# A selective-scan layer with a router: the sum over states as products of 512 moving columns in place of transposed blocks

## The reference

```python
resid_norm = resid * rsqrt(mean(resid * resid, -1) + EPS) * norm_w
skip = resid_norm @ W_skip                      # 512 -> 1024
x_in = resid_norm @ W_in                        # 512 -> 1024
x = silu(conv(x_in, 4 taps) + conv_b)
delta = softplus(x @ W_delta_1 @ W_delta_2 + b_delta_2)
Bm, Cm = x @ W_B, x @ W_C                       # 16 states each
def step(h, inp):                               # over the 2048 positions
    d_l, B_l, C_l, x_l = inp
    h = h * exp(d_l[:, :, None] * A) + (d_l * x_l)[:, :, None] * B_l[:, None, :]
    return h, einsum('ben,bn->be', h, C_l)      # the sum over states
y_skip = (y + x * W_D) * silu(skip)
return resid + y_skip @ W_out
```

## Time and profile before

| | |
|---|---|
| time before, median of 3 | 2380.34 us (2379.85 to 2382.69) |
| the profiled execution | 2379.91 us, its span 2378.0 us |
| PE busy | 1958.7 us (82%), 11717 records |
| POOL busy | 1913.5 us (80%) |
| DVE busy | 1795.4 us (75%) |
| ACT busy | 1669.1 us (70%) |
| mean granted clock of TensorE | 0.939 |
| DMA share | 56.9% of 16 engines |

### The profile page before, as it was taken

One profiled execution on the slowest core, in us unless ns is written; L12 is line 12 of the kernel. 1 busy time (PEld: TensorE's weight loads), 2 busy tenths in 40 slices (PEclk: granted clock), 3 DMA queues, 4 the chain that ended last, 5 costly groups with the idle time before them and its releaser, 6 DMA issues. The chain is left out here.

```text
span 2378.0 us, 35550 instructions
## 1 busy us (share of the span) xinstructions
PE 1958.7 (82%) x11717; PEld 1584.2 (67%) x11717; DVE 1795.4 (75%) x3105; ACT 1669.1 (70%) x3276; POOL 1913.5 (80%) x1192
## 2 busy tenths in 40 slices
PE   5577777898889898898889898898889988797883
PEld 3456666777667676777667686776667776666551
DVE  3377877798697977888697977889697887887522
ACT  2368686877769685787779686786868687787421
POOL 1279898898789797989879897998879898999512
PEclk9988988999999999999999999999999999999996
DMA  4555556665747565674657556574757646555320
GB/s 159 169 178 182 189 177 215 201 216 157 225 151 239 180 215 183 203 229 150 210 175 235 196 186 215 185 228 148 232 169 222 194 154 207 181 183 160 120 71 18
DMA packets 239281, 434.31 MB, mean 183 GB/s; under 512 B 19134, under 2 KB 135418, under 8 KB 239098
## 3 DMA queue, kind: packets, MB, share of 16 engines
q1 hardware_dynamic: 239098, 432.04, 56.9%
HBM read 347.57 MB, written 84.41 MB: 182 GB/s over the span
## 5 line engine op out<-in xcount | busy, mean ns | idle before, releaser
L608 POOL TENSOR_TENSOR hc<-h,c_all 128x1024 f32<-128x1024 f32 x512 | 1205.0, 2365 | 219.5 <-DVE h L953 160.0
L953 DVE TENSOR_TENSOR_SCAN h<-operand,carry,bank 128x512 f32<-128x512 f32 x480 | 597.1, 1271 | 174.1 <-PE bank L1129 142.7
L1134 PE MATMUL y_sum<-ident,hc 128*128 128x128 f32 x4096 | 624.7, 281 | 13.0 <-POOL hc L608 12.7
L1129 PE MATMUL bank<-ident,u_t 128*128 128x128 f32 x2560 | 417.3, 288 | 243.2 <-DVE h L953 219.7
L722 ACT ACTIVATE u_t<-dx_t,b_t 128x256 f32<-128x256 f32 x1280 | 575.0, 499 | 0.5 <-PE bank L1129 0.5
L1129 PEld LDWEIGHTS bank<-ident,u_t 128*128 128x128 f32 x2560 | 312.4, 148 | 375.1 <-issue 240.2
L1134 PEld LDWEIGHTS y_sum<-ident,hc 128*128 128x128 f32 x4096 | 506.1, 146 | 79.8 <-issue 50.2
L592 POOL TENSOR_TENSOR operand<-dx_q,b_all 128x1024 f32<-128x1024 f32 x192 | 454.5, 2367 | 11.0 <-DMA b_all<-bc_dram 11.0
L703 ACT ACTIVATE bank<-delta_q,neg_a 128x512 f32<-128x512 f32 x384 | 262.5, 684 | 263.1 <-DVE h L953 262.7
L703 ACT ACTIVATE operand<-delta_q,neg_a 128x512 f32<-128x512 f32 x640 | 432.9, 714 | 0.0
L953 DVE TENSOR_TENSOR_SCAN h<-bank,carry,operand 128x512 f32<-128x512 f32 x288 | 354.9, 1270 | 33.1 <-POOL operand L592 16.4
(11 more groups left out here) (124 smaller groups left out, 2009.3 us busy)
## 6 DMA issues: line engine op xcount, KB each, us to landing
c_all<-bc_dram SPq DMA_DIRECT2D x256, 512.0 KB, 4.3
b_all<-bc_dram SPq DMA_DIRECT2D x192, 256.0 KB, 5.2
win<-in_L_attn_W_in SPq DMA_DIRECT2D x64, 512.0 KB, 5.7
wskip<-in_L_attn_W_skip SPq DMA_DIRECT2D x64, 512.0 KB, 6.2
x_dram<-x SPq DMA_DIRECT2D x64, 256.0 KB, 4.5
delta_dram<-delta SPq DMA_DIRECT2D x32, 512.0 KB, 7.3
dx_dram<-dx SPq DMA_DIRECT2D x32, 512.0 KB, 7.3
delta_q<-delta_dram SPq DMA_DIRECT2D x32, 512.0 KB, 5.8
```

Source lines behind the costliest of these rows:

```text
L608: nc.gpsimd.tensor_tensor(hc[:, number % 3], h[:, number % 3], c_all[:, j % 2, s % 2:s % 2 + 1].to_broadcast([P, 2, SPAN]), ALU.mult).then ...
L953: nc.vector.tensor_tensor_scan(h[:, number % 3, q], first, second, start, ALU.mult, ALU.add).then_inc(scan_done.sem, 1)
L1129: last = transpose(bank[:, q, b * P:(b + 1) * P], u_t[:, j % 2, b, q * P:(q + 1) * P], ident[:])
L1134: return matmul(to, lhsT=of, rhs=ident[:], is_transpose=True, start=start, stop=stop, skip_group_check=True)
```

## The change

`y_sum` is kept in [e, l]. The identity is the stationary operand and hc moves, 512 columns for each q, as a plain product; x * W_D is the product of diag_d (stationary) with x_q, 512 columns. y_out and y_dram are in [e, l] too, so the part of a chunk is a slice of 256 positions, and `acc` needs no transposes any more: they go, with the signal `y_turned`. DVE writes the gate over the skip product in the bank `routed`, and `ys` is routed * acc; the SBUF tile `gate` goes. What waited for `gate_ready` on PE (the next pair's skip product, the transposes of h2 and dx into routed) now waits for `ys_ready`, as does SP's load of acc two pairs on. ACT's waits on gate_ready stay.

```diff
@@
-    y_dram = nc.dram_tensor("y_dram", [2, 2, PAIRS, P, TB, QE], F32).ap()
+    y_dram = nc.dram_tensor("y_dram", [2, PAIRS, P, 2, SPAN], F32).ap()
@@
-        acc = sb("acc", P, 2, TB, QE)
-        thg, gate = sb("thg", P, 2, 2, T), sb("gate", P, 2, 2, T)
+        acc = sb("acc", P, 2, 2, T)
+        thg = sb("thg", P, 2, 2, T)
@@ load_acc
-                    if v := due(sp, y_turned, t, p - 1):
-                        sp.wait_ge(y_turned.sem, v)
-                    sp.dma_start(acc[:, p % 2], y_dram[chunk // 2 % 2, chunk % 2, p]).then_inc(
+                    if v := due(sp, ys_ready, t, p - 1):
+                        sp.wait_ge(ys_ready.sem, v)
+                    sp.dma_start(acc[:, p % 2], y_dram[chunk // 2 % 2, p, :, :, chunk % 2 * T:(chunk % 2 + 1) * T]).then_inc(
                         acc_loaded[p % 2].sem, 16)
@@ store_y
-                    sp.dma_start(y_dram[stage % 2, :, quarter].rearrange("h p b e -> p h b e"),
-                                 y_out[:].rearrange("p (h b) e -> p h b e", h=2)).then_inc(y_stored.sem, 16)
+                    sp.dma_start(y_dram[stage % 2, quarter], y_out[:]).then_inc(y_stored.sem, 16)
@@ take_y
-                    for pair in range(2):
-                        part = slice(2 * pair, 2 * pair + 2)
-                        nc.scalar.activation(y_out[:, part], y_sum[:, part], ACT.Copy,
-                                             scale=0.5).then_inc(y_read.sem, 1)
+                    for q in range(2):
+                        nc.scalar.activation(y_out[:, q], y_sum[:, q], ACT.Copy, scale=0.5).then_inc(y_read.sem, 1)
@@ DVE, mix
-                                        if v := due(dve, ys_ready, t, p - 1):
-                                            dve.wait_ge(ys_ready.sem, v)
                                         nc.vector.scalar_tensor_tensor(
-                                            out=gate[:, p % 2].rearrange("p e t -> p (e t)"),
-                                            in0=thg[:, p % 2].rearrange("p e t -> p (e t)"), scalar=1.0,
+                                            out=routed[:], in0=thg[:, p % 2].rearrange("p e t -> p (e t)"), scalar=1.0,
                                             in1=routed[:], op0=ALU.add,
                                             op1=ALU.mult).then_inc(gate_ready.sem, 1)
-                                    if s == 3 * p + 16:
-                                        if v := due(dve, y_turned, t, p + 1):
-                                            dve.wait_ge(y_turned.sem, v)
+                                        if v := due(dve, acc_loaded[p % 2], t, p // 2 + 1):
+                                            dve.wait_ge(acc_loaded[p % 2].sem, v)
@@
                                         nc.vector.tensor_tensor(
-                                            ys[:, 2 * p:2 * p + 2, :].rearrange("p e t -> p (e t)"), mixed[:],
-                                            gate[:, p % 2].rearrange("p e t -> p (e t)"),
+                                            ys[:, 2 * p:2 * p + 2, :].rearrange("p e t -> p (e t)"), routed[:],
+                                            acc[:, p % 2].rearrange("p e t -> p (e t)"),
                                             ALU.mult).then_inc(ys_ready.sem, 1)
@@ add_y
-                        for b in (2 * pair, 2 * pair + 1):
-                            for q in range(2):
-                                last = matmul(y_sum[:, b, q * P:(q + 1) * P], lhsT=x_q[:, q, b * P:(b + 1) * P],
-                                              rhs=diag_d[:, 2 * quarter + q], start=b % 2 == 0 and q == 0,
-                                              stop=False, skip_group_check=True)
+                        last = matmul(y_sum[:, q], lhsT=diag_d[:, 2 * quarter + q], rhs=x_q[:, q], start=True,
+                                      stop=False)
@@
-                    for b in (2 * pair, 2 * pair + 1):
-                        for q in range(2):
-                            last = add_turned(y_sum[:, b, q * P:(q + 1) * P], hc[:, number % 3, q, b * P:(b + 1) * P],
-                                              False, n == N - 1)
+                    last = matmul(y_sum[:, q], lhsT=ident[:], rhs=hc[:, number % 3, q], start=False, stop=n == N - 1)
@@ PE, skip product
-                                    if v := due(pe, gate_ready, t, p):
-                                        pe.wait_ge(gate_ready.sem, v)
+                                    if v := due(pe, ys_ready, t, p):
+                                        pe.wait_ge(ys_ready.sem, v)
@@ PE, slot 3p + 15
-                                if s == 3 * p + 15 and not late:
...
-                                    for e in range(2):
-                                        for b in range(TB):
-                                            last = transpose(mixed[:, (2 * e + b) * P:(2 * e + b + 1) * P],
-                                                             acc[:, p % 2, b, e * P:(e + 1) * P], ident[:])
-                                    last.then_inc(y_turned.sem, 1)
```

More of the change, by code:

```diff
@@ L169, in build @@
         carry = sb("carry", P, N, ET)
-        y_out = sb("y_out", P, SB, QE)
-        acc = sb("acc", P, 2, TB, QE)
-        thg, gate = sb("thg", P, 2, 2, T), sb("gate", P, 2, 2, T)
+        y_out = sb("y_out", P, 2, SPAN)
+        acc = sb("acc", P, 2, 2, T)
+        thg = sb("thg", P, 2, 2, T)
         ys = sb("ys", P, ET, T)
@@ L187, in build @@
         bank = stack.enter_context(nc.psum_tensor("bank", [P, 2, SPAN], F32))
-        y_sum = stack.enter_context(nc.psum_tensor("y_sum", [P, SB, QE], F32))
+        y_sum = stack.enter_context(nc.psum_tensor("y_sum", [P, 2, SPAN], F32))
         mixed, routed = (stack.enter_context(nc.psum_tensor(n, [P, 512], F32)) for n in ("mixed", "routed"))
@@ L239, in build @@
         gate_ready = signal("gate_ready", "mix", PAIRS)
-        y_turned, ys_ready = signal("y_turned", "mix", PAIRS), signal("ys_ready", "mix", PAIRS)
+        ys_ready = signal("ys_ready", "mix", PAIRS)
         xp_loaded, z0_ready = loads_of("xp_loaded", "mix", 1), signal("z0_ready", "mix", TB)
@@ L1131, in turn_u, with add_y @@
                     last.then_inc(ut_turned.sem, 1)
-                def add_turned(to, of, start, stop):
-                    return matmul(to, lhsT=of, rhs=ident[:], is_transpose=True, start=start, stop=stop,
-                                  skip_group_check=True)
-                def add_y(t, s, pair):
+                def add_y(t, s, q):
                     if not (now := slot_of(t, s)):
@@ L1143, in add_y @@
                     if n == 0:
-                        if t == -FIRST and k == 0 and pair == 0:
+                        if t == -FIRST and k == 0 and q == 0:
                             pe.wait_ge(diag_made, ET)
@@ L1147, in add_y @@
                             pe.wait_ge(xq_loaded.sem, v)
-                        if v := due(pe, y_read, t, 2 * k - 2 + pair + 1):
+                        if v := due(pe, y_read, t, 2 * k - 2 + q + 1):
                             pe.wait_ge(y_read.sem, v)
-                        for b in (2 * pair, 2 * pair + 1):
-                            for q in range(2):
-                                last = matmul(y_sum[:, b, q * P:(q + 1) * P], lhsT=x_q[:, q, b * P:(b + 1) * P],
-                                              rhs=diag_d[:, 2 * quarter + q], start=b % 2 == 0 and q == 0,
-                                              stop=False, skip_group_check=True)
-                        if pair:
+                        last = matmul(y_sum[:, q], lhsT=diag_d[:, 2 * quarter + q], rhs=x_q[:, q], start=True,
+                                      stop=False)
+                        if q:
                             last.then_inc(xq_read.sem, 1)
@@ L1174, in turn_dx @@
                     if k:
-                        for read, step in ((gate_ready, t - 1), (o_ready, t - 1)):
+                        for read, step in ((ys_ready, t - 1), (o_ready, t - 1)):
                             if v := due(pe, read, step, read.per):
@@ L1319, in side_work @@
                                         last.then_inc(skip_done.sem, 1)
-                                if s == 3 * p + 15 and not late:
-                                    if v := due(pe, acc_loaded[p % 2], t, p // 2 + 1):
-                                        pe.wait_ge(acc_loaded[p % 2].sem, v)
-                                    if v := due(pe, z_ready, t - 1, TB):
-                                        pe.wait_ge(z_ready.sem, v)
-                                    if p and (v := due(pe, ys_ready, t, p)):
-                                        pe.wait_ge(ys_ready.sem, v)
-                                    for e in range(2):
-                                        for b in range(TB):
-                                            last = transpose(mixed[:, (2 * e + b) * P:(2 * e + b + 1) * P],
-                                                             acc[:, p % 2, b, e * P:(e + 1) * P], ident[:])
```

(3 more changed lines are left out.)

4 lines of the change are left out of this document (2 added, 2 removed).

## The result

The changed kernel takes 2530.0 us, median of 4 (2527.5 to 2533.4), against 2380.1 us: a ratio of 1.063 (95% interval 1.061 to 1.065), 150 us slower. Forecast were 2558 us (2462 to 2675), slower with a chance of 0.93. The profiled execution has a span of 2529.4 us, 151.4 more than the span before.

A forecast was written before the change was run, and what follows sets the result against it. PE was taken to bound five of eight stretches of a step, DVE, ACT and POOL the others. Twelve full steps 141, first and last steps 32, end 5: 178 us; 2378 + 178 + 2 = 2558 us, range 2462 to 2675.

The forecast's parts named there:

- The size of a state: Sum over states on PE: 0.87 us removed and 1.72 added per state, 0.85 us more each, 435 us in the run.
- The spill-over, stretch by stretch: Quiet step, eight stretches of four states: added PE work beyond each stretch's idle time lengthens the step, 13.5 us taken.
- the lower of my two estimates: Quiet step: spill-over of 11.4 us with PE's work counted by starts, against 16.5 with full stretches taken as full.
- The steps with the wait for dx_q: Every other step: the last stretch's extra 3.4 us lies in PE's wait for dx_q, so 10 us a step, 60 for six.
- First and last steps: First two and last two steps: PE has less to do, so 6 us each and 10 us each, 32 in all.
- The end: After the last scan: PE's skip product waits for ys, 0.8 us later for each of two chunks x three pairs, 5 us.
- Acc's transposes: PE, slots 15, 18, 21 and 24: 256 records go, 0.44 us in each slot, 1.7 a step, 28 us in all.
- The gate: DVE's gate written into the bank routed: nothing taken, at most 3 us; PE's later start rarely waits in the scanned part.
- Hidden anyway: Rival, whole run: PE's idle time hides the added work, 2358 to 2385 us; chance 0.07.
- Nothing covered: Rival, whole run: scans wait in light stretches too, so none of the added PE work is hidden, 2792 us; chance 0.10.
- A full clock: Rival, PE's clock: products replacing transposes keep it at its upper level, 54 us less than the forecast, 2504; chance 0.10.

The follow-up runs named there:

- double_turned: The kernel before, with each state's eight accumulating transposes issued twice; 2546.0 us, ratio 1.071.
- double_light: The kernel before, with the accumulating transposes doubled only for the states of slots 5 to 10, where TensorE was idle; 2381.3 us, ratio 1.000.
- double_full: The kernel before, with the accumulating transposes doubled only for the states of slots 12 to 17, where TensorE showed 98 to 100% busy; 2428.8 us, ratio 1.020.
- after_dx25: The kernel after, with the loads of delta_q and dx_q issued at SP's slot 25 instead of 27 in odd steps; 2498.3 us, ratio 1.049.
- sum_only: The kernel after, with the gate in its SBUF tile again and PE's skip products waiting for the gate instead of ys; 2541.2 us, ratio 1.067.
- after_filled: The kernel after, with twelve transposes of the identity behind each skip product of the last two chunks; 2523.2 us, ratio 1.061.
- half_columns: The kernel after, with the sum over states taking only the first 256 of each 512 columns; 2389.2 us, ratio 1.003.
- second dose: The kernel after, with each 512-column product of the sum preceded by one of 256 columns more; 2830.1 us, ratio 1.189.

## Why the prediction was right

*The size of a state.* 0.87 us removed, 1.72 added: the starts after show 0.86 for two records. Right, and double_turned shows that this time is what counts, whatever it is spent on.

*The spill-over, stretch by stretch.* Forecast for a quiet step were +3.4, 1.9, 0, 2.8, 3.0, 2.0, 0 and 3.4, reduced by the slack in full stretches to 13.5; the means measured are +2.5, 2.1, 0, 1.4, 2.9, -0.2, 0.2 and 2.8, together 11.7. The mechanism holds: double_light and double_full show that cover in one stretch is no cover for another. The sizes are off in three places. In stretch 6 ACT and POOL set the pace, and PE had room for all of its 3 us, though it was shown 94% busy: 2.2 us. A stretch shown full has gaps: 0.9 in the first and 0.6 in the eighth. And in stretch 4 the clock rose: 1.4. At the clock of the kernel before that stretch takes 18.5 us instead of 15.6, which is near the 2.8 forecast; on average over the twelve full steps it took 17.0. I had left the clock as it was. That the step came out near the lower of my two estimates (11.4, by the work counted by starts) is in part luck, as that estimate has the same 0.85 us off in each stretch, and the measured one has nearly half of its difference in stretch 6. With 13.5 I had gone somewhat less than half way to the other.

*The steps with the wait for dx_q.* Forecast +10, measured +8.1 (140.6 to 148.7). With the quiet steps this makes +113 for the twelve full steps against 141 forecast, which is the term of the sum that was mis-sized, and as much as the 28 us between forecast and time. Some 16 us of it are the clock in stretch 4 (an estimate: 2.8 forecast less 1.44 measured, 12 times). after_dx25 shows the cover by the wait: without it 21 us of the sum's price come back.

*First and last steps.* Forecast 12 and 20, measured 6.7 and 14.9: 10 us too many.

*The end.* Forecast 5, measured 14.7, 10 us too few. This and the error before it cancel, which is luck. The 0.8 us a pair for ys is there (ys at 2399.51, the product at 2400.34), six times; sum_only, without it, is 5.5 us shorter, but has two slow products fewer and slower ys as well. Not foreseen was that longer idle times between pairs let the clock fall; after_filled took 7.7 us back. Nor was the sum's own time behind the last scan counted: double_turned, in which the waits of this part are as before, is 3.5 us longer there than the kernel before.

*Acc's transposes.* Counted at 1.7 us a step and in the forecast by 0.44 in each of four stretches: measured 1.6 in a quiet step and 18 of 28 us in all. Right in size, but it shows in two of the four stretches.

*The gate.* The price of the write is 8 ns. In the scanned part no wait for ys is seen (17.2 us in 6 waits in all, at the end), as forecast: PE is late itself. half_columns shows the waits that arise when PE isn't: 24.8 us in the scanned part.

*The rivals.* Hidden anyway: excluded. Nothing covered: excluded, the change cost 37% of its 407 us net. It comes nearer for a second dose (300 of 440 us). A full clock: right in part. The mean granted clock rose from 0.939 to 0.964, so that about 182 us of the span are at the lower level instead of 290 (an estimate: twice the missing share, by the span). Where PE is full the rise was worth what it gave back: stretch 4 takes 15.5 us at 1.00, 17.2 at 0.92 and 18.5 at 0.88, and grew by 1.4 us a step instead of 2.8. But the clock was full throughout in one of five quiet steps only, and the 54 us of this rival supposed it in all; about 16 us came. double_turned has the same rise with transposes alone, so it came from PE being idle less, and not from the kind of instruction.

## What to carry to other kernels

Price an edit on an engine in each stretch between two points at which the engines are tied together, not by its idle share of the run: the same 84 us of work cost 0 in one place and 48 in another. Before a window stands for its kind, lay it beside its neighbours: the quiet step read here was the one in five with a full clock, and 1.7 us shorter in one stretch for that. A transposed fp32 block of 128 columns holds TensorE here for half of what a plain fp32 product of the same block does (0.109 against 0.215 us), so a layout that saves 16 transposes a step by turning 256 others into plain products loses. And look at the waits that every kernel shares: moving one pair of loads ahead by two slots gave 53 us (2328 us), while no arrangement of the sum tried here was faster than the one of the kernel before.

## What the runs showed of the hardware

With two fp32 inputs in SBUF (sum_only) a DVE product of 512 columns took 691 to 2776 ns beside a busy POOL, and 690 to 693 with one of them in PSUM (the kernel after), in 64 instructions each. Where it started during a product of POOL it took 2.22 us and POOL's next one 2.81; where it started ahead of POOL's it took 0.69 and POOL's 2.56. TensorE's clock was at its upper level in stretches in which most of its records were transposes, and with the sum's transposes doubled the mean granted clock rose from 0.939 to 0.970. With TensorE full, the same work of four states took 15.5 us at a granted clock of 1.00, 17.2 at 0.92 and 18.5 at 0.88. After the last scan, filling the pauses of 2.3 us between products with transposes brought four of five shown products back to 3.7 us, from 5.4 to 6.2 in four of six.
